# Staged query and key projections, spread to their operand tiles by DMA, with a new job table around them

## The reference, cut to what matters

```python
x = x + tanh(g_xattn) * xattn(layernorm(x), ctx, Wq, Wk, Wv, Wo, bo)
x = x + tanh(g_ffn)   * experts(layernorm(x), gate_w, expert_w, expert_b)

# xattn: qh = q @ Wq, kh = kv @ Wk, vh = kv @ Wv, split into 16 heads of 64
attn = softmax(einsum('bhnd,bhmd->bhnm', qh, kh) * 64 ** -0.5)
out  = einsum('bhnm,bhmd->bhnd', attn, vh) @ Wo + bo
# experts: probs = softmax(xt @ gate_w.T); top 2; out = sum_e comb[:, e] * (xt @ expert_w[e].T + expert_b[e])
```

## Time and profile before

| | |
|---|---|
| median of 3 runs | 1213.2 us (1208.41 to 1215.2) |
| the profiled execution's own time | 1210.17 us |
| its span, first to last instruction | 1208.5 us |
| PE busy | 1135.7 us (94%) |
| DVE busy | 979.0 us (81%) |
| ACT busy | 849.6 us (70%) |
| POOL busy | 648.0 us (54%) |
| mean granted TensorE clock | 0.989 of full speed |

### The profile page before, as it was taken

How to read it: one execution, slowest core, us unless ns; L and a number is a source line. 1 busy time by engine, 2 the same in 40 slices (tenths; PEclk the granted TensorE clock), 3 DMA queues, 4 the chain that set the end, 5 groups by cost and what they waited for, 6 DMA issues and landing times.

```text
span 1208.5 us, 30873 instructions
## 1 busy us (share of the span) xinstructions
PE 1135.7 (94%) x10592; PEld 913.4 (76%) x10592; DVE 979.0 (81%) x1945; ACT 849.6 (70%) x1531; POOL 648.0 (54%) x579
## 2 busy tenths in 40 slices
PE   4888999999999999999899999999999999999968
PEld 3677777788778887788777887778877788778846
DVE  7788878987898778987789877898778887897646
ACT  4888888676876678676786768867687677866610
POOL 2566666455655547455564545645556455654610
PEclk8999999999999999999999999999999999999979
DMA  4333212122221122221222112211122121121000
GB/s 133 78 85 79 37 37 54 29 37 45 37 53 29 28 54 36 46 37 27 57 37 45 28 37 45 54 36 28 41 50 45 28 37 40 33 37 36 2 19 17
DMA packets 97521, 51.79 MB, mean 43 GB/s; under 512 B 77000, under 2 KB 86608, under 8 KB 97360
## 3 DMA queue, kind: packets, MB, share of 16 engines
q1 hardware_dynamic: 97360, 49.74, 20.3%
HBM read 11.68 MB, written 4.19 MB: 13 GB/s over the span
## 4 chain that ended last, share of the span: by engine, by line
PE 70%; DVE 15%; issue 7%; DMA 3%; ACT 3%; SPq 1%; DVEq 0%; POOL 0%; ACTq 0%
PE MB L934 30%; PE PV L1057 12%; PE MX L1037 8%; PE ST L1047 7%; PE ST L1044 7%; DVE nmax L767 3%; DVE KA L744 3%; PE MB L944 3%; DMA QB<-nmax 2%; DVE QB L739 1%; PE MB L1014 1%; DVE stats L656 1%; DVE w L879 1%; SPq L432 1%; DVE m L886 1%
## 5 line engine op out<-in xcount | busy, mean ns | idle before, releaser
L514 POOL TENSOR_TENSOR p_s<-pf,p_s 128x512 f16<-128x512 f32 x512 | 594.7, 1169 | 496.1 <-ACT p_s L621 492.5
L596 ACT ACTIVATE pf<-ST 128x512 f32<-128x512 f32 x512 | 306.2, 599 | 193.0 <-PE ST L1047 186.3
L767 DVE TENSOR_REDUCE nmax<-MX 128x1 fp32r<-128x512 f32 x512 | 347.2, 685 | 69.0 <-PE MX L1037 60.9
L621 ACT ACTIVATE p_s<-pf 128x512 f16<-128x512 f32 x512 | 318.1, 629 | 45.1 <-PE PV L1057 42.0
L1037 PE MATMUL MX<-KA,QA 128*128 128x512 f32 x512 | 216.9, 426 | 18.6 <-DVE nmax L767 15.2
L1057 PEld LDWEIGHTS PV<-v_s,p_s 128*128 128x128 f16 x6144 | 193.6, 98 | 33.6 <-issue 24.7
L1047 PE MATMUL ST<-QB,KB 65*128 65x512 f32 x512 | 204.8, 400 | 7.2 <-DMA QB<-nmax 7.0
L1057 PE MATMUL PV<-v_s,p_s 128*128 128x65 f16 x6144 | 209.0, 194 | 1.3 <-POOL p_s L514 1.3
L1044 PE MATMUL ST<-QA,KA 128*128 128x512 f32 x512 | 206.2, 403 | 3.6 <-ACT pf L596 3.1
L934 PE MATMUL MB<-ex_s,x2t_s 128*128 128x512 f32 x708 | 188.8, 402 | 3.2 <-DVE KA L744 3.2
L934 PEld LDWEIGHTS MB<-ex_s,x2t_s 128*128 128x128 f32 x708 | 128.1, 188 | 34.9 <-DVE KA L744 6.3
(11 more groups left out here) (120 smaller groups left out, 1113.4 us busy)
## 6 DMA issues: line engine op xcount, KB each, us to landing
QA<-QA SPq DMA_DIRECT2D x64, 256.0 KB, 3.0
KB<-KA SPq DMA_DIRECT2D x64, 256.0 KB, 3.0
QB<-nmax SPq DMA_DIRECT2D x512, 0.5 KB, 1.9
xin<-x SPq DMA_DIRECT2D x8, 512.0 KB, 4.0
out<-acc SPq DMA_DIRECT2D x8, 512.0 KB, 3.2
kvin<-kv_t SPq DMA_DIRECT2D x8, 256.0 KB, 4.2
acc<-expert_t SPq DMA_DIRECT2D x8, 256.0 KB, 3.3
acc<-wo SPq DMA_DIRECT2D x4, 256.0 KB, 3.3
```

Source lines behind the costliest of these rows:

```text
L514: pool.tensor_tensor(p_s[:, h % 2, 1, t, :], pf[:, t, :], p_s[:, h % 2, 0, t, :], ALU.subtract)\
L596: act.activation(pf[:, t, :], st_bank(h, t)[:, :], ACT.Exp, bias=P_SHIFT, scale=SCALE)\
L621: act.activation(p_s[:, h % 2, 0, t, :], pf[:, t, :], ACT.Copy).then_inc(p_hi, 1)
L767: dve.tensor_reduce(nmax[:, h % 2, t:t + 1], MX[t % 2][:, :], AX.X, ALU.max, negate=True)\
```

## The change

q and k are no longer written straight into their operand tiles. ACT writes one 128x512 hi part and DVE one 128x512 lo part into the staging tiles `q_hl` and `k_hl` (one buffer each, hi at index 0, lo at index 1), and SP spreads them by DMAs of 64 partitions x 512: four for `QA` (two in each of two units), four for `KA` (two in each of two units), and, during the even head before the pair is used, two for `QB` in unit 0 and two for `KB` in unit 1. `QB` and `KB` have slots for two pairs. The next q or k may be written only when the copies of the one before have landed (new waits on ACT and DVE). The pairs 0 and 1 of the first batch are made in the old way (`copy_early` is the old `copy`).

The table moves jobs: for pairs 2 to 5 q stands in unit 2 and k in unit 3 of the even head; `("v", 2, 0)` goes to (0, 1), both `("wo", 3, j)` one unit earlier, `("ot", 0)` one later, the router one later, the logits from (5, 1) to (5, 2), the routing steps one unit later, the statistics of the second layer norm from (3, 0) to (2, 3), and the last two expert jobs from (15, 0) and (15, 3) to (14, 3) and (15, 0).

```diff
-    (2, 1): [("wo", 3, 0)], (2, 2): [("wo", 3, 1)], (2, 3): [("q", 3)],
...
+    (2, 0): [("wo", 3, 0)], (2, 1): [("wo", 3, 1)], (2, 2): [("q", 3)], (2, 3): [("k", 3)],
...
-    (15, 0): [("expert", 3, 2)], (15, 1): [("wo", 2, 1)], (15, 2): [("ot", 6)], (15, 3): [("expert", 3, 3)],
...
+    (15, 0): [("expert", 3, 3)], (15, 1): [("wo", 2, 1)], (15, 2): [("ot", 6)],
...
-LN2_AT, LN2_APPLY_AT = (3, 0), (3, 2)
+LN2_AT, LN2_APPLY_AT = (2, 3), (3, 2)
...
-LOGITS_AT = (5, 3)
-ROUTE_SLOTS = [(5, 3), (6, 0), (6, 1), (6, 2), (6, 3), (7, 0)]
+LOGITS_AT = (6, 0)
+ROUTE_SLOTS = [(6, 0), (6, 1), (6, 2), (6, 3), (7, 0), (7, 1)]
...
-        QB = sb("QB", [P, 2 * SLOTS, TOKENS], F32R)
+        QB = sb("QB", [P, 4, TOKENS], F32R)
...
-        KB = sb("KB", [P, 2 * SLOTS, TOKENS], F32R)
+        KB = sb("KB", [P, 4, TOKENS], F32R)
+        q_hl = sb("q_hl", [P, 2, TOKENS], F32R)
+        k_hl = sb("k_hl", [P, 2, TOKENS], F32R)
...
-            def copy(it, name):
+            def copy_early(it, name):
+                kind, p = name
...
+                sp.wait_ge(job_hi, it.done(HI, name))
...
+            def copy_first(it, name, part):
...
-                sp.wait_ge(job_hi, it.done(HI, name))
...
+                if kind == "q":
+                    if part == 0:
+                        sp.wait_ge(job_hi, it.done(HI, name))
+                    rows = slice(HEAD * part, HEAD * (part + 1))
+                    sp.dma_start(QA[0:HEAD, s + part, :].bitcast(F32), q_hl[rows, 0, :].bitcast(F32))\
+                      .then_inc(qa_in[p % 2], 16)
+                    sp.dma_start(QA[HEAD:P, s + part, :].bitcast(F32), q_hl[rows, 0, :].bitcast(F32))\
+                      .then_inc(qa_in[p % 2], 16)
+                else:
+                    if part == 0:
+                        sp.wait_ge(job_hi, it.done(HI, name))
+                    else:
+                        sp.wait_ge(job_free, it.done(JOBS, name) + BANKS)
+                    to = slice(HEAD * part, HEAD * (part + 1))
+                    sp.dma_start(KA[to, s, :].bitcast(F32), k_hl[0:HEAD, part, :].bitcast(F32))\
+                      .then_inc(ka_in[p % 2], 16)
+                    sp.dma_start(KA[to, s + 1, :].bitcast(F32), k_hl[HEAD:P, part, :].bitcast(F32))\
+                      .then_inc(ka_in[p % 2], 16)
+            def copy_second(it, h, kind):
+                p = h // 2 + 1
+                dst, src, copied = (QB, q_hl[:, 1, :], qb_in) if kind == "q" else (KB, k_hl[:, 0, :], kb_in)
+                if kind == "q":
+                    sp.wait_ge(st_ready, tile_count(it.b, h - 1, TT - 1))
+                for i in range(2):
+                    sp.dma_start(dst[0:HEAD, 2 * (p % 2) + i, :].bitcast(F32),
+                                 src[HEAD * i:HEAD * (i + 1), :].bitcast(F32)).then_inc(copied[p % 2], 16)
...
-                sp.dma_start(QB[HEAD:HEAD + 1, it.head_slot(h), t * P:(t + 1) * P].bitcast(F32),
+                sp.dma_start(QB[HEAD:HEAD + 1, h % 4, t * P:(t + 1) * P].bitcast(F32),
...
+                    second = h % 2 == 0 and not (it.kind == FIRST and h == 0) and \
+                        not (it.kind == LAST and h == HEADS - 2)
+                    if second and t == 0:
+                        copy_second(it, h, "q")
...
-                    for name in taken_in(it.kind, h, t):
-                        if name[0] in "qk":
-                            copy(it, name)
+                    if second and t == 1:
+                        copy_second(it, h, "k")
+                    for kind, part, later in (("q", 0, 1), ("q", 1, 2), ("k", 0, 2), ("k", 1, 3)):
+                        n = h * TT + t - later
+                        for name in taken_in(it.kind, n // TT, n % TT) if n >= 0 else []:
+                            if name[0] == kind:
+                                copy_first(it, name, part)
...
-                if kind in ("q", "k"):
+                if kind in ("q", "k") and it.kind != PRO:
+                    p = name[1]
+                    if name == ("q", 2):
+                        act.wait_ge(job_free, it.start(JOBS) + BANKS)
+                    elif kind == "q":
+                        act.wait_ge(job_free, it.done(JOBS, ("q", (p - 1) % PAIRS)) + BANKS)
+                    before = p - 1 if p >= 2 else p - 1 + PAIRS
+                    if not early_pair(it, before):
+                        if kind == "q":
+                            act.wait_ge(qa_in[before % 2], qa_count(it, before))
+                        else:
+                            act.wait_ge(ka_in[before % 2], ka_count(it, before))
+                            act.wait_ge(kb_in[before % 2], kb_count(it, before))
+                    last = act.activation((q_hl if kind == "q" else k_hl)[:, 0, :], m[:, :], ACT.Copy)
+                elif kind in ("q", "k"):
...
-                if kind == "q":
+                if kind in ("q", "k") and it.kind != PRO:
+                    p = name[1]
+                    before = p - 1 if p >= 2 else p - 1 + PAIRS
+                    hl = q_hl if kind == "q" else k_hl
+                    if not early_pair(it, before):
+                        if kind == "q":
+                            dve.wait_ge(qb_in[before % 2], qb_count(it, before))
+                        else:
+                            dve.wait_ge(ka_in[before % 2], ka_count(it, before))
+                    last = dve.tensor_tensor(hl[:, 1, :], m[:, :], hl[:, 0, :].bitcast(F32), ALU.subtract)
+                elif kind == "q":
...
-                p, ahead = h // 2, (h + 2) // 2 % PAIRS
+                p = h // 2
...
-                    pe.wait_ge(k_dup[p % 2], dup_count(b, p))
+                    pe.wait_ge(kb_in[p % 2], kb_count(it, p))
+                    if not early_pair(it, p):
+                        pe.wait_ge(qb_in[p % 2], qb_count(it, p))
...
-                                pe.wait_ge(job_free, (it.done_before if ahead == 1 else it.done)(JOBS, ("k", ahead))
-                                           + BANKS)
-                                pe.wait_ge(q_dup[ahead % 2], dup_count(b if ahead else b + 1, ahead))
+                                following = h // 2 + 1
+                                if early_pair(it, following):
+                                    pe.wait_ge(job_free, it.start(JOBS) + BANKS)
+                                else:
+                                    pe.wait_ge(ka_in[following % 2], ka_count(it, following))
+                                pe.wait_ge(qa_in[following % 2], qa_count(it, following))
```

38 lines of the change are left out of this document (25 added, 13 removed), and 12 rows, old and new, of the table PLACED.

## The result

| | before | after |
|---|---|---|
| median | 1214.2 us (1208.41 to 1218.2) | 1249.4 us (1246.85 to 1254.9) |
| profiled span | 1208.5 us | 1250.0 us |
| DVE, ACT busy | 979.0, 849.6 us | 880.2, 769.4 us |
| mean granted clock | 0.989 | 0.978 |

After is slower: its time is 1.029 of before's, interval 1.0255 to 1.0329. The forecast was 1187; the rival "copies bind, slower" had said 1248.

A forecast was written before the change was run, and what follows sets the result against it. PE was taken as the bound, DVE second in the first ten heads. A gain of 2.8 us in each of seven batches (20 us) plus 5 in the first took 1210.2 to 1185, 1187 us as median; range 1160 to 1218.

The forecast's parts named there:

- copies bind, slower: Rival, chance 0.15: `KA` copies landing 4.3 us behind the row's end cost four places 3 us each; 1248 us.
- The bound and the size of the instructions: PE bounds, DVE second in heads 0 to 9; one 128-partition instruction replaces two at half cost, 0.69 and 0.59 us.
- The table: New job order: removes two waits a batch, for `o_n` and the k job; shortens head 1 by 0.70 us.
- SP and the landing: SP is slowest in odd heads, 1.65 us a unit, 6.6 a head; a 128 KB copy lands in 2.5 us.
- The four places: Where rows and copies make PE wait; all waits of a batch 9.2 us before, 6.4 after, gain 2.8.
- (a): (1, 0): rows of head 1 behind store, `kvin` load and two `QB` copies; 1.4 us in place of 0.9.
- (b): (2, 0): row's way 2.9 us, up to 1.1 more, against 2.8 us of PE work; 1.2 us of wait.
- (c): (4, 0) and (4, 2): rows, then last `KA` copies needing 4.1 us against PE's 4.5; 1.0 us for both.
- (d): Waits elsewhere in the batch: 0.3 us.
- The first batch: Less ACT and DVE work, but copies late more often; gain of 5 us, ends 0 and 10.
- The clock: Full in every window of the loop and PE's work unchanged, so nothing was charged.

## Why the prediction was wrong, step by step

**The bound and the size of the instructions: right.** PE bounds both kernels. The new instructions took 687 and 598 ns (0.69 and 0.59 forecast), DVE ended at 880 us (893 forecast) and ACT at 769 (776). The waits for `o_n` and the k bank went, and heads 6 and 7 took 19.06 us, a little over half way from 20.50 to the forecast 18.

**The table: wrong.** It was charged nothing but a shorter head 1. Alone it costs 20 us. It also moves more than the text ahead of the prediction lists: in heads 5 to 7 `("v", 2, 1)`, `("ot", 1)`, `("wo", 0, j)`, `("ot", 2)` and `("expert", 0, 1)` change units as well.

**SP and the landing: right but for a size.** SP issued without a pause for the length of head 3, at 1.9 us and more a unit where 1.65 was counted, and the landings took 2.3 to 2.4 us where 2.5 was taken. By the estimate from the Trainium skill, *DMA: Bandwidth & Descriptors*, "Anatomy of one DMA", 128 KB land in 2.3 us; the page gives that fit for DMAs that GpSimd issues. The median landings of after, issued by SP, agree:

```profile
QA<-q_hl SPq DMA_DIRECT2D x248, 128.0 KB, 2.4
KA<-k_hl SPq DMA_DIRECT2D x248, 128.0 KB, 2.3
QB<-nmax SPq DMA_DIRECT2D x512, 0.5 KB, 2.0
```

**The four places: this is the step that failed.** They and the rest were to lose 6.4 us a batch instead of 9.2, a gain of 2.8; the loop lost 3.4 us more a batch instead. (a) was taken at 1.4 and lost 2.5: the last row of head 1 was issued 3.0 to 5.9 us after its reduction, mostly near 3.9, behind store, load and copies; before, mostly 1.0. That is 2.8 more where I had counted 1.1 for the issues. Its landing, for which I had counted another 1.1, got no longer: 2.0 to 3.6 us, before 2.1 to 3.5. (b) was taken at 1.2 and lost 0.67. (c) was taken at 1.0 for (4, 0) and (4, 2) together and lost 1.27 + 1.77. I had PE busy for 4.5 us from the issue of the row of (3, 3) to the matmul of (4, 2), on the ground that the short gap of 2.16 us before came from a late DVE, which the change would mend. In after the row is issued at 494.93 and the matmul could have started at 496.96: 2.0 us again, and 2.0 to 2.3 in all six batches of the loop.

The premise was wrong, and the trace of before could have shown it: DVE stood idle there, for ACT (0.51 us before, 2.05 after). The rows of both kernels, from the matmul of (3, 3) (468.46 before, 490.01 after) to its reduction, the first of the x2:

```profile
468.64 2.07 ACT L627 ACTIVATE xn<-acc,shift,rstd 128x256 f32<-128x256 f32 x4
471.09 0.59 ACT L559 ACTIVATE ot_s<-MB 128x512 fp32r<-128x512 f32 x1
471.71 0.69 DVE L754 TENSOR_TENSOR ot_s<-MB,ot_s 128x512 fp32r<-128x512 f32 x1 [0.51 <-ACT ot_s L559]
472.32 1.28 DVE L767 TENSOR_REDUCE nmax<-MX 128x1 fp32r<-128x512 f32 x2
```
```profile
490.09 2.08 ACT L702 ACTIVATE xn<-acc,shift,rstd 128x256 f32<-128x256 f32 x4
492.55 0.67 ACT L638 ACTIVATE v_s<-MB,v_mul 128x512 f16<-128x512 f32 x1
493.26 0.75 DVE L842 SCALAR_TENSOR_TENSOR v_s<-MB,v_mul,v_s 128x512 f16<-128x512 f32 x1 [2.05 <-ACT v_s L638]
493.93 1.28 DVE L852 TENSOR_REDUCE nmax<-MX 128x1 fp32r<-128x512 f32 x2
```

ACT applies the second layer norm for 2.1 us, the hi part of a job comes behind it, DVE's lo part waits for that hi part, and the reduction stands behind the lo part. So it ended 4.5 us after its matmul had started before, and 4.6 after, in all six batches; and in five of the six SP issued the row 0.03 us later (0.3 in the one shown). Less work on DVE only made DVE's wait longer, and SP's own copies did not delay this row. No run moved the layer norm, so this cause is read from the traces and was not tried; with the copies one unit earlier the reduction ended at 4.6 us still. A short gap tells who is late only when the late engine's own wait has been looked up.

(d), all other places, was taken at 0.3; (0, 2), (2, 2), (6, 2) and (7, 0) alone lost 4.0, 3.0 more than before. The first three wait for `KA` by the very mechanism that I had written down for (4, 2) and not carried to its neighbours, and (7, 0) waits for a row behind the `xin` load and two copies, a place that the prediction did not look at.

**The first batch: wrong sign.** 5 us of gain forecast, 12.8 of loss measured. "The copies are late more often" was in the text, without a price. Waits of PE there:

```profile
PE ST L1132 <- DMA QB<-nmax: 7.8, 7, 2.4
PE MX L1122 <- DMA KA<-k_hl: 7.5, 5, 2.8
```

Before, the rows cost 3.3 us there. That is 12 us more of waiting for DMAs; less waiting for DVE gave some back, and the clock took about 5.

**The clock: charged nothing, and it wasn't nothing.** PE in heads 0 and 1 of the fifth batch of after (timeline: start, length, line, tile, count, idle before):

```profile
606.32 1.62 PE L1142 MATMUL PV<-v_s,p_s 128*128 128x65 f16 x48
...
617.98 0.79 PE L1132 MATMUL ST<-QB,KB 65*128 65x512 f32 x1 [3.42 <-DMA QB<-nmax]
618.56 0.63 PE L1122 MATMUL MX<-KA,QA 128*128 128x512 f32 x1
618.99 2.73 PE L1142 MATMUL PV<-v_s,p_s 128*128 128x65 f16 x48
```

These are the same kind of 48 matmuls, of unit (0, 0) and of unit (1, 0): 1.62 us undisturbed, 2.73 behind a wait of 3.42 us. A matmul of 512 columns took 0.79 and 0.63 instead of 0.40 there. The granted clock was 0.50, its lower level, 1.2 GHz; the window of that stretch, columns as in the earlier trace rows:

```profile
618.02:621.43 3.41, 3.41 (x46) 2.89 (x47) 1.66 (x3) 1.60 (x3) 0.71 (x1) 0.50 0.36 67
```

The wait cost its idle time and about 1.7 us more, from start to start. This was not one case. In the eight batches of after the trace has nine such stretches, each beginning within 1.6 us of the end of a wait of 1.5 to 4.4 us, 31 us in all; the eight batches of before have one, of 3.4 us. (Other waits of up to 2.1 us passed without one.) By batch, the granted clock was 0.95 in the first against 0.99 before, 0.99 in the loop against 1.00, and 0.98 in the last against 1.00. Summed over the matmuls of these stretches, against the same ones at the full clock, my estimate is 15 us in after and under 2 in before: some 13 of the 41 us are the clock's share of the new waits. The forecast had this term at nothing, because PE's work stayed the same; it was PE's pauses that changed.

**The rival that came true.** Its number, 1248, is within the runs of after. Its kind was right: copies land late for L1037 of (h, 2), and rows queue. Its point of decision was not: it asked for a `KA` landing 4.3 us behind the row's end, and 498.49 less 495.47 is 3.0. The waits came at 3.0 because PE's own work there is 2.0 and not 4.5. They were smaller than the 3 us each that it priced; the table, rows at (1, 0) and (7, 0) and the clock made up the difference, so that its number fits is in part luck. The chance of 0.15 rested on the same 4.5 us.

## What to carry to other kernels

When a change trades work of a full engine for DMAs of an engine that issues in order, write that engine's issues out in a row for the tightest stretch, everything in them (rows, copies, loads, stores), and compare each landing with the reader's earliest start if nothing else is late; do it at every place of the same form and in the first turn of the loop too. One unit of schedule for the copies gave back 32 of 35 us here. Before you blame a late engine for a short gap, look up what that engine waited for. Give new waits a price for the clock as well. And issue time is a resource by itself, here 0.4 to 0.6 us for a DMA whatever it carried, to be spent on the engine that has it free at that stage.

## What the runs showed of the hardware that I had not expected

A row of 0.5 KB landed in 1.9 to 2.0 us when alone and in 4.0 to 4.3 behind a 512 KB load and two copies. A copy within the on-chip memory landed in 1.8 us for 16 KB, 2.3 for 128 KB and 3.0 for 256 KB (medians), so eight times the bytes cost 0.5 us. The issue of a 128 KB copy cost 0.62 us on ACT and 0.54 to 0.60 on SP (medians), that of the 512 KB load of `xin` 0.38; single issues of copies took up to 1.8 us on SP. And after one wait of 3.4 us the clock was at 1.2 GHz, and the next matmuls of 512 columns took 0.79 and 0.63 us instead of 0.40.
